# A two-layer graph attention kernel: the GpSimd gathers without scratch memsets between them, and in another order behind the adjacency stream

## The reference

```python
h = relu(layernorm(x))
scores = where(adj > 0, h @ weight @ input.T, NEG_PAD)
x = x + softmax(scores / 0.07, axis=1) @ input            # layer one
h = relu(layernorm(x)) @ W
e = leaky_relu((h @ a_src)[:, None] + (h @ a_dst)[None, :], 0.2)
att = softmax(where(valid, e, NEG), axis=1)               # valid: adj > 0 and the column of h not all cancelled
att = where(att >= 1e-4, att, 0) * n_valid                # and 0 where a row's top share is not over 1e-4
x = x + elu(h + att @ h)                                  # layer two
```

## Time and profile before

| what | value |
|---|---|
| median of three runs | 715.66 us |
| span of the profiled execution (first to last instruction) | 713.4 us |
| median less that span | 2.26 us |
| POOL busy | 370.8 us (52%) |
| DVE busy | 506.1 us (71%) |
| ACT busy | 407.4 us (57%) |
| PE busy | 393.6 us (55%) |

### The profile page before, as it was taken

One profiled execution on the slowest core, in us unless ns is written; L12 is line 12 of the kernel. 1 busy time (PEld: TensorE's weight loads), 2 busy tenths in 40 slices (PEclk: granted clock), 3 DMA queues, 4 the chain that ended last, 5 costly groups with the idle time before them and its releaser, 6 DMA issues.

```text
span 713.4 us, 9730 instructions
## 1 busy us (share of the span) xinstructions
PE 393.6 (55%) x2916; PEld 270.0 (38%) x2947; DVE 506.1 (71%) x2125; ACT 407.4 (57%) x424; POOL 370.8 (52%) x425
## 2 busy tenths in 40 slices
PE   3244465576767575859576756754702601526653
PEld 1011133253535362626253534453601500516653
DVE  0009778898989897979798989898307313559985
ACT  6348496777989888797988988622201100022222
POOL 5000060606161525243377877788787887888800
PEclk9557697978979888888999999875655555657788
DMA  8999989999898999898999999511111221114322
GB/s 326 412 425 419 367 312 418 333 374 364 295 413 318 412 343 410 331 398 338 389 366 386 399 404 400 204 56 43 53 44 46 57 87 46 42 54 120 110 67 92
DMA packets 37480, 186.79 MB, mean 262 GB/s; under 512 B 7856, under 2 KB 8112, under 8 KB 18864
## 3 DMA queue, kind: packets, MB, share of 16 engines
q1 hardware_dynamic: 28208, 167.02, 60.2%
q0 software_dynamic: 9216, 19.11, 9.1%
HBM read 179.73 MB, written 6.37 MB: 261 GB/s over the span
## 4 chain that ended last, share of the span: by engine, by line
DVE 44%; POOL 25%; issue 12%; PE 7%; DMA 5%; ACT 5%; DVEq 0%; SPq 0%; POOLq 0%
POOL arena L823 14%; DMA arena<-in_adj 5%; PE K L1433 5%; POOL mean_w L818 4%; DVE keys L1033 3%; DVE G L1144 3%; ACT R_all L906 2%; DVE RTp L1203 2%; ACT arena L877 2%; POOL E L823 2%; POOL X L794 2%; DVE cand L1063 2%; DVE mi_w L1184 2%; POOL arena L794 1%; DVE cand L1051 1%
## 5 line engine op out<-in xcount | busy, mean ns | idle before, releaser
L877 ACT ACTIVATE arena<-arena,half_c 128x2048 fp8e4<-128x2048 int32 x144 | 281.2, 1997 | 35.8 <-DMA arena<-in_adj 28.1
L794 POOL DMA_INDIRECT X<-in_L_gnn_input,idx_all x132 | 131.3, 994 | 255.1 <-DVE idx_near L1115 217.2
L1433 PE MATMUL K<-arena,bits 128*128 128x512 fp8e4 x576 | 167.6, 431 | 50.0 <-ACT arena L877 24.8
L823 POOL DMA_INDIRECT arena<-table,idx_near x96 | 104.2, 1085 | 28.5 <-issue 22.3
L1433 PEld LDWEIGHTS K<-arena,bits 128*128 128x128 bf16 x576 | 59.2, 108 | 93.4 <-ACT arena L877 30.1
L1033 DVE MAX8 keys<-K 128x8 int32<-128x128 f32 x192 | 42.4, 281 | 55.4 <-PE K L1433 55.3
L823 POOL DMA_INDIRECT E<-table,idx_near x48 | 47.3, 985 | 14.4 <-issue 12.2
L1445 PE MATMUL G<-g,R_all 128*128 128x128 bf16 x324 | 28.2, 243 | 39.0 <-DVE G L1144 24.8
L1445 PEld LDWEIGHTS G<-g,R_all 128*128 128x128 fp8e4 x324 | 23.3, 110 | 48.8 <-issue 28.2
L906 ACT CAST R_all<-G 128x512 fp8e4<-128x512 f32 x36 | 19.8, 587 | 34.4 <-PE G L1467 20.6
L818 POOL MEMSET mean_w<- 128x512 f32 x72 | 38.4, 533 | 2.1
(11 more groups left out here) (249 smaller groups left out, 1016.2 us busy)
## 6 DMA issues: line engine op xcount, KB each, us to landing
arena<-in_adj SPq DMA_DIRECT2D x144, 1024.0 KB
table<-hs SPq DMA_DIRECT2D x12, 262.0 KB, 8.3
hs<-table SPq DMA_DIRECT2D x12, 262.0 KB, 2.7
E<-in_L_gnn_input SPq DMA_DIRECT2D x1, 3072.0 KB, 25.8
out_x<-x_all SPq DMA_DIRECT2D x12, 256.0 KB
x_all<-in_x SPq DMA_DIRECT2D x1, 2560.0 KB, 19.5
X<-in_L_gnn_input,idx_all POOLq DMA_INDIRECT x132, 5.7
arena<-table,idx_near POOLq DMA_INDIRECT x96, 2.5
```

The costliest lines, as they stand in the source:

```text
L794: pool.indirect_dma_start(out=x_of(b)[:, e, :], out_offset=None, in_=inp, in_offset=bass.IndirectOffsetOnAxis(ap=idx_all[:, at:at + 1], ax ...
L823: pool.indirect_dma_start(out=E[g][:, t, :], out_offset=None, in_=tables[g], in_offset=bass.IndirectOffsetOnAxis(ap=idx_near[:, t, g:g + 1 ...
L877: nc.scalar.activation(sign[:, load % RING, :], ring[:, load % RING, :], ACT.Sign, bias=half_c[:], scale=1.0, saturate=False).then_inc(sig ...
L1433: last = mm(bank_[:], bits[:, third * TB + j, :], sign[:, load % RING, j * FOLD:(j + 1) * FOLD], start=False, stop=(third == G - 1 and j = ...
```

## The change

The pauses between table gathers go. In the list behind the stream, the last block's neighbours are asked for right after `add_mean` of block 10, as soon as their index is there; then come the four remaining gathers of third 0, all 48 of third 1, and all 48 of third 2. The wait on `folded` moves behind the neighbours (their index can only be there once the stream is folded).

```diff
@@ records @@
                         ).then_inc(E_r[g][t // Q], 16)
-                        if t % FEW == FEW - 1:
-                            pause()
@@ behind the loop over the stream's blocks @@
-                pool.wait_ge(folded, T * G)
                 scale_mean(NB - 2)
                 add_mean(NB - 2)
-                third_stored(1)
-                records(1, 0, 2 * Q)
                 neighbours(NB - 1, 0, BG // 2)
                 scale_mean(NB - 1)
                 add_mean(NB - 1)
                 neighbours(NB - 1, BG // 2, BG)
-                records(1, 2 * Q, 5 * Q)
                 records(0, FROM[NB - 1], T)
+                pool.wait_ge(folded, T * G)
+                third_stored(1)
+                records(1, 0, T)
                 third_stored(2)
-                records(2, 0, 2 * Q)
-                records(1, 5 * Q, T)
-                records(2, 2 * Q, T)
+                records(2, 0, T)
```

More of the change, by code:

```diff
@@ L437, in fast_path @@
     LP = LW + 1
-    FEW = 4
     REC = D + 3
@@ L813, in add_mean @@
                     pool.wait_ge(mean_added, b + 1)
-                def pause():
-                    for _ in range(2):
-                        link(pool.memset(mean_w[:], 0.0))
                 def records(g, first, last):
```

## The result

The changed kernel took 697.27 us, median of 4 runs (693.09 to 701.91), against 715.5 us: a ratio of 0.974, 95% interval 0.969 to 0.979. The forecast was 695.3, in a range of 689 to 706. The profiled execution took 697.16 us with a span of 695.5. Two further sets of five runs gave medians of 698.8 and 698.3.

The account below looks back on a forecast made before the run. POOL's list of gathers bounds the kernel behind the stream until `take(2)`, then VectorE's steps: 19.6 + 0.5 - 1.3 = 18.8 us, and 1.6 more, off a 713.4 us span gives 693.0; plus 2.26, 695.3 us, range 689 to 706.

Parts of the forecast that it names:

- The pauses: POOL's list before `take(2)`: 18 pauses of 1.09 us go, 19.6 us gained, with gathers keeping to 1.25 us.
- hidden anyway: Rival: memsets ran while the queue caught up, so without them gathers wait for it; 714 to 716 us, chance 0.05.
- the queue falls behind: Rival: POOL fills the queue's room in third 1, then each gather waits for an earlier one; slower, chance 0.07.
- The start: First gather behind the last block's index, after a 2 us wait: at 493.2 us, 0.5 us earlier than before.
- the order moves the end by nothing: Earlier neighbours buy 24 us of a chain with 27 us to spare; only the pauses gain.
- Stalls: Gathers before `take(2)` held by VectorE operations with two SBUF operands: four at 1.45 us plus smaller, 6.3 us, 1.3 more.
- The last block: Block 11's score starts at about 513.6 us, table 2 is ready at 552, POOL comes to it at 579.
- Behind `take(2)`: From `take(2)` to the end: POOL needs 12.9 us for a step's gathers, DVE 15.2, so POOL stays ahead.
- The 1.57 us wait: DVE's wait for data at 678.97 us in the old trace, behind `take(2)`; forecast to go.
- fewer stalls: Rival: gathers seldom start inside large VectorE operations, 3 to 4 us of stalls go; 692 us, chance 0.10.
- DVE's 11.0 us: DVE's time from `take(1)` complete to ready for `take(2)`'s last part: ready at 611.6, before the data at 613.2.
- The rival in which VectorE waits: Layer two's copies wait for POOL's gathers, steps of 16 us or more; at worst 704 us, half 700, chance 0.14.

Follow-up runs that it names:

- fill_wait: The changed kernel, but four gathers of third 1 are issued before POOL waits for the last block's index; 693.05 us, ratio 0.968.
- order_only: The changed kernel's new list, with the old kernel's pauses left in; 716.11 us, ratio 1.001.
- by_steps: The changed kernel with four third 1 gathers before the index wait, and thirds 1 and 2 in turns of eight from tile 32; 683.9 us, ratio 0.957.
- again: The changed kernel, unedited, measured once more; 698.79 us, ratio 0.975.

## Why the prediction was right

*The pauses.* Forecast 19.6 us for 18 of them; between the same order with and without them, 20.9 us (138.4 less 117.5) up to `take(2)`, or 21.3 on POOL's list alone, of which 1.7 us are longer gathers (88.3 against 86.6 us busy for the 88) and not pauses. The price of one, and that nothing is won back in it, hold over a factor of four in length. But for those beside VectorE's two-operand operations, the gathers kept to 1.25 us in a run of a hundred; "hidden anyway" and "the queue falls behind" are both out.

*The start.* Forecast 493.2, measured 496.49. This term of the sum was mis-sized, by 3.3 us. 2.1 of these are the later stream. The relief at L1112 came, but POOL's elementwise instructions met others of DVE's operations (L1142 took 0.90 us beside them, 0.16 to 0.34 in the other blocks), and the index stood 31.9 us behind the stream's end instead of 32.2: 0.3 us were won, not 0.9. And from the end of L1104 to the gather were 0.79 us, not 0.27. The wait that I put at 2 us was 5.3, and `fill_wait` shows that it counts in full: the sentence that the order moves the end by nothing holds with pauses (`order_only`, 1.001), and without them the order costs 4 to 5 us; for a list that follows layer two it doesn't hold either, since `by_steps` uses the time that the early neighbours buy.

*Stalls.* Forecast 6.3 us, measured 3.5: the 88 gathers from 496.49 to 612.0 us were busy 86.6 us, less 88 x 0.945. The large products of blocks 10 and 11 cost 1.46 and 1.05 us (gathers of 2.40 at 506.38 and 1.99 at 530.31), the first of step 1 0.68, as the gather met its last half, and the second met one only behind the last that `take(2)` needs (612.29). Of the later ones most cost the whole (2.41 us at 627.21). The 2.41 us that the forecast calls the longest gather in the trace of before isn't quite that, 2.48 is (at 637.88); only the price of a rival hangs on it.

*The last block.* Forecast: score at 513.6, table at 552, POOL there at 579, 27 us to spare. Measured 516.69, 555.07 and 580.97: 26 us to spare. That the early neighbours buy time in a chain that isn't late was right for this list, and `order_only` shows it.

*Behind `take(2)`.* Forecast 79.8 us, measured 81.5. The 1.57 us wait did go, and the steps were shorter than 15.2 us (14.9 and 14.6 from one L1344 to the next). But step 2 itself took 16.2: DVE now comes to it without a pause for data, and waits 0.81 and 1.31 us for TensorE, whose work before had been done while DVE waited for gathers.

*Sum.* Forecast 20.4 us; the three medians moved by 18.2, 16.9 and 17.4, and the three profiles, counted behind the stream, by 20.0, 19.8 and 17.6. The gain is the pauses, as forecast: taken out of the old order they bring 22.2 us (715.69 to 693.5), and the new order takes 4 to 5 of these back, which the forecast put at nothing. That the sum came out so near is in part luck: up to `take(2)` a start 1.2 us later behind the stream stands against stalls 2.8 us smaller, and behind `take(2)` 1.7 us are missing. The 2.26 us for time outside the span are too much as well; in every recorded execution it is 1.5 to 2.1 us, in the profiled one 1.66.

Of the rivals, "fewer stalls" came in part: with 2.8 us less of them, DVE's 11.0 us from `take(1)` set `take(2)`, as that rival says, where the forecast had POOL's list set it 1.6 us behind DVE. The time doesn't show it, as the start was later. The rival in which VectorE waits didn't come: copies beside gathers still took 0.4 us here and there, and the steps were no longer for it.

## What to carry to other kernels

When one engine's list of instructions sets the time, filler in that list costs its full length, and an instruction that waits costs whatever stands behind it: put work that is ready in front of the wait, as `fill_wait` did. Starting a chain sooner is worth nothing while it has time to spare; ask what consumes the list's results first, and order the list by that (`by_steps` took 9 us less than `fill_wait` with the same gathers, and there the early start counted). An engine's idle time in the old trace can hide another engine's lag: what was a wait for data becomes in part a wait for the next-slowest.

## What was not expected of the hardware

POOL's instructions can hold up small operations of VectorE. In the changed kernel an operation on 128x8 elements, which took 0.17 us in three of the twelve blocks and 1.7 in nine, began beside one of POOL's gathers and ended only with the elementwise instruction behind it (469.40); a second one, 0.17 or 1.11 us, ended with the next (470.76):

```profile
467.71 1.72 DVE L1173 TENSOR_TENSOR mi_w<-mi 128x8 f32<-128x8 f32 x1
...
469.68 1.11 DVE L1175 TENSOR_TENSOR mi<-mi_w,mi 128x8 bf16<-128x8 f32 x1
```
```profile
467.39 0.94 POOL L793 DMA_INDIRECT X<-in_L_gnn_input,idx_all  x1 [0.30 <-issue]
468.35 1.05 POOL L804 TENSOR_TENSOR mean_w<-mean_b,empty_all 128x512 f32<-128x512 f32 x1
469.48 1.28 POOL L810 TENSOR_TENSOR x_all<-x_all,mean_w 128x512 f32<-128x512 f32 x1
```

What they meet depends on POOL's timing. The last block's index came 30.4 us behind the stream's end with half a pause, 31.9 to 32.3 in the three profiles of the changed kernel. That such meetings make this difference is not shown: in `again` the later of them, at L1142, is missing, and the index came at 32.3 all the same. Why the stream ends anywhere between 459.6 and 468.3 us wasn't looked into. Between the first two profiles of the changed kernel it is 4.2 of the 4.4 us in the span; between the first and the third, whose stream ended 0.6 us sooner and whose span is 1.8 us longer, it explains nothing.
